# Inverse sums as powers on GpSimd, layer normalisation as scale and bias on ScalarE, and a table of orders with later hand-overs

## The reference

```python
s1 = q1 @ k1.T * scale + mask;  s2 = q2 @ k2.T * scale + mask        # 16 heads, 1024 x 1024, causal
a1, a2 = softmax(s1), softmax(s2)
lam = exp(sum(lq1 * lk1)) - exp(sum(lq2 * lk2)) + LAMBDA_INIT
out = (a1 - lam * a2) @ v                                            # per head, 64 wide
out = (out - mean) * rsqrt(var + 1e-5) * gn_w + gn_b                 # per head, over all positions
x = layernorm(x + out * (1 - LAMBDA_INIT) @ Wo)                      # (x - m) / sqrt(v + 1e-5)
x = layernorm(x + (silu(x @ wu.T) * (x @ wg.T)) @ wd.T)              # ternary wu, wg, wd
```

## Time and profile before

| | |
|---|---|
| median of 3 runs | 2446.61 us (2437.75 to 2449.0) |
| profiled execution | 2448.3 us, its span 2446.5 us |
| TensorE's mean granted clock | 0.976 of full speed |
| instructions | 41259 |
| HBM read, written | 182.53 MB, 71.30 MB, 104 GB/s over the span |
| DMA packets | 257603, mean 105 GB/s |

### The profile page before, as it was taken

How to read it: one execution, slowest core, us unless ns; L and a number is a source line. 1 busy time by engine, 2 the same in 40 slices (tenths; PEclk the granted TensorE clock), 3 DMA queues, 4 the chain that set the end, 5 groups by cost and what they waited for, 6 DMA issues and landing times.

```text
span 2446.5 us, 41259 instructions
## 1 busy us (share of the span) xinstructions
PE 2257.5 (92%) x13602; PEld 1401.3 (57%) x13602; DVE 1851.3 (76%) x4406; ACT 1417.7 (58%) x3466; POOL 860.1 (35%) x1330
## 2 busy tenths in 40 slices
PE   7799998898899999999899999999899999988999
PEld 4456655465556666666566666565565665643444
DVE  3577888888888888878788888888788888762343
ACT  1467755465556767667566766666567677640231
POOL 0344376758432323323222324324222233220132
PEclk9899999899999999999999999999999999998999
DMA  6757565466533122212622222213431211113000
GB/s 225 231 169 228 185 203 168 148 184 194 176 121 100 44 63 73 78 52 66 190 81 71 68 63 87 83 40 108 143 83 53 65 47 54 40 64 109 1 18 18
DMA packets 257603, 256.53 MB, mean 105 GB/s; under 512 B 31344, under 2 KB 199408, under 8 KB 255216
## 3 DMA queue, kind: packets, MB, share of 16 engines
q1 hardware_dynamic: 246016, 220.26, 29.8%
q10 hardware_dynamic: 11376, 33.63, 4.4%
HBM read 182.53 MB, written 71.30 MB: 104 GB/s over the span
## 4 chain that ended last, share of the span: by engine, by line
PE 66%; DVE 13%; issue 6%; POOL 6%; DMA 6%; ACT 3%; SPq 1%; ACTq 0%; DVEq 0%; POOLq 0%
PE F L994 15%; PE PV L936 9%; PE S L919 8%; PE F L1003 8%; PE F L981 8%; PE F L964 7%; PE F L904 7%; DVE e_long L1237 3%; DVE e_long L1326 3%; PE PV L939 2%; POOL coef L1170 1%; DVE e_short L1326 1%; POOL x_lo L1210 1%; PE F L972 1%; DMA wt<-in_w_up 1%
## 5 line engine op out<-in xcount | busy, mean ns | idle before, releaser
L1055 ACT ACTIVATE e_long<-e_long,nmax 128x768 f32<-128x768 f32 (+3 forms) x512 | 505.2, 989 | 148.8 <-DVE nmax L1237 144.2
L1170 POOL TENSOR_SCALAR coef<-lsum,linv,neglam 128x1 f32<-128x1 f32 x512 | 248.1, 486 | 929.4 <-DVE linv L1322 928.6
L919 PE MATMUL S<-kstk,qstk 128*128 128x384 f32 (+5 forms) x1536 | 510.1, 427 | 61.0 <-DVE nmax L1237 51.8
L1237 DVE CUSTOM_DVE_ANT_0 e_long<-S,mask_b 128x768 f32<-128x768 f32 (+3 forms) x512 | 512.7, 1018 | 68.7 <-PE S L919 64.7
L919 PEld LDWEIGHTS S<-kstk,qstk 128*128 128x128 f32 x1536 | 280.4, 195 | 208.3 <-DVE nmax L1237 89.4
L1048 ACT ACTIVATE dt_long<-F 128x512 f32<-128x512 f32 (+3 forms) x512 | 239.6, 512 | 272.8 <-PE F L904 271.9
L1326 DVE SCALAR_TENSOR_TENSOR e_long<-e_long,coef 128x1024 f32<-128x1024 f32 (+3 forms) x256 | 295.8, 1155 | 35.2 <-POOL coef L1170 34.0
L1055 ACT ACTIVATE e_short<-e_short,nmax 128x384 f32<-128x384 f32 (+3 forms) x512 | 283.3, 556 | 65.4 <-DVE nmax L1237 63.0
L964 PE MATMUL F<-xT,wr 128*128 128x512 f32 x640 | 314.5, 624 | 3.5 <-issue 0.7
L1237 DVE CUSTOM_DVE_ANT_0 e_short<-S,mask_b 128x384 f32<-128x384 f32 (+3 forms) x512 | 238.6, 486 | 44.3 <-PE S L919 43.0
L981 PE MATMUL F<-wo_sb,at_sb 128*128 128x512 f32 x512 | 240.9, 606 | 33.2 <-DMA at_sb<-da 26.4
(11 more groups left out here) (105 smaller groups left out, 3207.5 us busy)
## 6 DMA issues: line engine op xcount, KB each, us to landing
qstk<-dq SPq DMA_DIRECT2D x512, 128.0 KB, 2.8
dq<-hl SPq DMA_DIRECT2D x32, 1024.0 KB, 4.8
wr<-in_w_proj ACTq DMA_DIRECT2D x48, 512.0 KB, 4.1
kstk<-dk SPq DMA_DIRECT2D x64, 256.0 KB, 5.3
da<-ra SPq DMA_DIRECT2D x32, 512.0 KB, 3.1
at_sb<-da SPq DMA_DIRECT2D x32, 512.0 KB, 4.1
x<-in_x SPq DMA_DIRECT2D x16, 512.0 KB, 6.3
dk<-hl SPq DMA_DIRECT2D x8, 1024.0 KB, 7.0
```

The source lines that it names most:

```text
L919: last = nc.tensor.matmul(slot[:, h, :], qstk[:, duo % 4, 2 * r + m, :].bitcast(F32R), kstk[:, g % 2, m, h * w:(h + 1) * w].bitcast(F32R), ...
L1055: nc.scalar.activation(e, e, ACT.Exp, bias=nmax[:, u % 8:u % 8 + 1], scale=-1.0, accum_out=lsum[:, n % 4, m:m + 1]).then_inc(s_exp, 1)
L1170: nc.gpsimd.tensor_scalar(coef[:, a % 2:a % 2 + 1], lsum[:, a % 4, 0:1], linv[:, a % 8, 1:2], neglam[:, :], ALU.mult, ALU.mult).then_inc(s ...
L1237: nc.vector.tensor_tensor_reduce(out, slot, mask, -1.0, -NEG, ALU.add, ALU.min, nmax[:, u % 8:u % 8 + 1]).then_inc(s_negmax, 1)
```

## The change

The reciprocal of the two row sums leaves DVE. POOL's `factor` now waits for the second exponent itself, takes both sums to the power -1 (128 x 2, with the exponents from a new tile `powers`, of which `mhalf` is now the first column) and waits for its own result; then it makes the coefficient as before. `reciprocal` and its semaphore are gone. The normalisation leaves DVE too: POOL's `rsqrt` also makes bias = -mean x inverse in place of the mean, and ACT computes x x inverse + bias with `Identity`. DVE's `variance` now waits for the normalisation four tiles back, which it had behind it in its own queue before. In the tables `HAND_OVER` grows for all four engines, `factor`, `normalise` and `rsqrt` get their new durations, and the items move to their new lists.

```diff
-HAND_OVER = {"pe": 0.2, "act": 0.12, "dve": 0.1, "pool": 0.12}
+HAND_OVER = {"pe": 0.3, "act": 0.5, "dve": 0.2, "pool": 0.4}
...
     if what == "factor":
-        return 0.67 if STEPS[a].r else 0.36
+        return 1.45 if STEPS[a].r else 1.15
...
-            "lambda": 0.3, "reciprocal": 0.1, "normalise": 0.48, "high": 0.63, "product": 0.22, "moments": 1.55,
+            "lambda": 0.3, "normalise": 0.65, "high": 0.63, "product": 0.22, "moments": 1.55,
...
-            "hidden low": 1.32, "rsqrt": 1.1, "rotate": 2.9, "low": 2.6, "group": 2.9, "less": 2.9}.get(what, 0.06)
+            "hidden low": 1.32, "rsqrt": 1.5, "rotate": 2.9, "low": 2.6, "group": 2.9, "less": 2.9}.get(what, 0.06)
...
-    elif what == "reciprocal":
-        out = [ITEM("exponent", a, 1)]
...
     elif what == "factor":
-        out = [ITEM("reciprocal", a), ITEM("minus lambda")]
+        out = [ITEM("exponent", a, 1), ITEM("minus lambda")]
...
-AHEAD = {"minimum": 1.0, "exponent": 1.0, "evict": 1.5, "inverses": 1.0, "factor": 2.0, "reciprocal": 0.8, "combine": 0.6, "empty": 3.0, "copy": 2.0,
+AHEAD = {"minimum": 1.0, "exponent": 1.0, "evict": 1.5, "inverses": 1.0, "factor": 2.0, "combine": 0.6, "empty": 3.0, "copy": 2.0,
...
-        mhalf = sb("mhalf", [P, 1])
+        powers = sb("powers", [P, 4])
+        mhalf, mone = powers[:, 0:1], powers[:, 2:4]
...
+                elif what == "normalise":
+                    i = LN[a]
+                    t = a.i if a.kind == "wo" else 4 * a.h + a.j
+                    act.wait_ge(s_rstd, i + 1)
+                    nc.scalar.activation(x1[:, t, :], x1[:, t, :], ACT.Identity, bias=lmv[:, i % 4, 0:1],
+                                         scale=lrs[:, i % 4:i % 4 + 1]).then_inc(s_ln, 1)
...
-                    pool.wait_ge(s_linv, a + 1)
+                    pool.wait_ge(s_exp, 2 * a + 2)
+                    link(nc.gpsimd.tensor_tensor(linv[:, a % 8, :], lsum[:, a % 4, :], mone, ALU.pow))
...
-                    nc.gpsimd.tensor_tensor(lrs[:, i % 4:i % 4 + 1], veps, mhalf[:, :], ALU.pow).then_inc(s_rstd, 1)
+                    link(nc.gpsimd.tensor_tensor(lrs[:, i % 4:i % 4 + 1], veps, mhalf, ALU.pow))
+                    mean = lmv[:, i % 4, 0:1]
+                    nc.gpsimd.tensor_scalar(mean, mean, lrs[:, i % 4:i % 4 + 1], -1.0, ALU.mult, ALU.mult).then_inc(s_rstd, 1)
...
                 freed(dve, job)
+                if i >= 4:
+                    dve.wait_ge(s_ln, i - 3)
...
-            def normalise(job):
-                i = LN[job]
-                t = job.i if job.kind == "wo" else 4 * job.h + job.j
-                dve.wait_ge(s_rstd, i + 1)
-                nc.vector.tensor_scalar(x1[:, t, :], x1[:, t, :], lmv[:, i % 4, 0:1], lrs[:, i % 4:i % 4 + 1],
-                                        ALU.subtract, ALU.mult).then_inc(s_ln, 1)
...
-                elif what == "reciprocal":
-                    dve.wait_ge(s_exp, 2 * a + 2)
-                    nc.vector.reciprocal(linv[:, a % 8, :], lsum[:, a % 4, :]).then_inc(s_linv, 1)
```

More of the change, by code:

```diff
@@ L390 @@
             *[[ITEM("copy", j) for j in OF_KIND[kind]] for kind in ("xT", "V", "x1T", "up")],
-            [ITEM("hidden", j) for j in OF_KIND["gate"]], [ITEM("sum", i) for i in range(PREP)],
+            [ITEM("hidden", j) for j in OF_KIND["gate"]], [ITEM("normalise", j) for j in LN_JOBS], [ITEM("sum", i) for i in range(PREP)],
             [ITEM("load x", i) for i in range(len(X_JOBS) - X_FIRST)], [ITEM("load w", i) for i in range(len(WLOADS))]],
-    "dve": [[ITEM("minimum", n, m) for n, m in _maps], [ITEM("reciprocal", n) for n in _heads],
+    "dve": [[ITEM("minimum", n, m) for n, m in _maps],
             [ITEM("combine", n) for n in _heads], [ITEM("product", duo) for duo in range(DUOS)],
@@ L396 @@
               for kinds in ("EO", ("x1T",), ("up", "gate"), ("wo", "y"))],
-            [ITEM("normalise", j) for j in LN_JOBS], [ITEM("high", j) for j in O_JOBS[ROT_FIRST:]],
+            [ITEM("high", j) for j in O_JOBS[ROT_FIRST:]],
             [ITEM(what, c) for c in range(CHUNKS) for what in ("moments", "spread", "deviation")],
@@ L725, in layer_kernel @@
         s_exp = sem("s_exp")
-        s_linv = sem("s_linv")
         s_coef = sem("s_coef")
@@ L1161, in _ @@
             assert made[0] == N_CONST
-            link(nc.gpsimd.memset(mhalf[:, :], -0.5))
+            link(nc.gpsimd.memset(mhalf, -0.5))
+            link(nc.gpsimd.memset(mone, -1.0))
             pool.wait_ge(s_gn, 16)
@@ L1197, in _ @@
                     pool.wait_ge(s_gve, a + 1)
-                    link(nc.gpsimd.tensor_tensor(gsm[:, 4:5], gsm[:, 3:4], mhalf[:, :], ALU.pow))
+                    link(nc.gpsimd.tensor_tensor(gsm[:, 4:5], gsm[:, 3:4], mhalf, ALU.pow))
                     link(nc.gpsimd.tensor_tensor(gsm[:, 5:6], gsm[:, 4:5], gn_sb[:, 0, c:c + 1], ALU.mult))
@@ L1329, in _ @@
                     empty(a)
-                elif what == "normalise":
-                    normalise(a)
                 elif what == "high":
```

## The result

| | |
|---|---|
| before, beside it | 2447.38 us median of 4 runs |
| changed kernel | 2403.19 us median of 4 runs (2401.43 to 2406.22) |
| ratio | 0.9829, 95% interval 0.9801 to 0.9856 |
| predicted | 2426, range 2398 to 2464 |

The account below looks back on a forecast made before the run. TensorE was taken as the bound, busy 2257.5 of 2446.5 us. Terms -13 - 7 - 2 + 9 - 8 + 0.6 = -20.4 us took the 2446.6 us median to 2426, range 2398 to 2464 for 8 in 10.

Parts of the forecast that it names:

- VectorE's relief: TensorE's waits for VectorE shrink with its load: -13 us in 700 to 2180, -7 in 300 to 700, -2 in 76 to 300.
- The table, -8 forecast: Larger hand-over numbers remove short waits of instructions planned just in time: -8 us, bounds -20 and +15.
- under 12: Sign of being right: TensorE's waits for the row maxima in 700 to 2180 fall under 12 us.
- rival (b): No change: later coefficients take back what the minima gained, ports take 41 us of VectorE's saving; 2434 to 2459, chance 0.25.
- GpSimd, +9 forecast: In 300 to 700 GpSimd gets 75 us more, 84% busy, delaying coefficients: +28 us at most, a third taken, +9.
- the 0.64 taken: Duration in us assumed for GpSimd's power on 128x2, between bounds 0.58 and 0.88.
- rival (c): Slower: GpSimd becomes the gate in 300 to 700, comparisons of weights queue with factors; 2478 us, chance 0.20.
- 3 us are spare: Long heads' second-map loop takes 4.8 us, two heads come every 7.9; this hides the 0.45 us longer path if orders use it.
- Contention: GpSimd's powers slow VectorE operations with two SBUF inputs: 25 ns per combine taken, 13 us in all, 41 kept for the range.
- the slope of 80 ns for 17 points: Combines' lengthening with GpSimd's load, 154 ns for 34 points, gives 80 ns for the powers' 17: 41 us of VectorE.
- the forecast's upper end: Sign of being right: VectorE's busy time falls from 1851.3 us to between 1735 and 1776.
- The normalisation, part of the relief: Moving it saves VectorE 35.1 us and 14.4 of waiting; ScalarE's instruction taken at 0.77 us, 49 us in all.

Follow-up runs that it names:

- spare reciprocal: Changed kernel, lists the same, plus one unneeded one-column reciprocal on VectorE behind each second row maximum: 2406.8 us, ratio 0.9826.
- the run with the measured factor: Changed kernel with the factor planned at its profiled duration, 1.3 and 1.6 us in place of 1.15 and 1.45: 2406.3 us, ratio 0.9818.
- The multiply: Changed kernel, lists the same, with a multiply in place of GpSimd's power, so its output is not the reference's: 2386.2 us, ratio 0.9747.
- the double power: Changed kernel, lists the same, with each power on GpSimd done twice: 2525.1 us, ratio 1.0308.

## Why the prediction was right or wrong

The sign and the range held. The time fell by twice the forecast, and the largest terms stood for the wrong cause. That the waits they counted fell by 19.5 us, near their 22, is luck: the table did it, not VectorE's relief.

**The table, -8 forecast, -17 measured** alone and -20 on top of the moves (2422.7 to 2403.2). The mechanism was named in part: VectorE's idle time in front of the reciprocals fell from 87.1 us to 47.3 with the table alone. What it had wrong is which waits the table removes. It looked at those of the scores for the maxima, and they stayed (51.8 and 53.8 us). Those of the transposes for the long maps, counted under VectorE's relief, fell by 14, most of it in 300 to 700. Over the span, before and with the table alone:

```profile
PE F L904 <- DVE e_long L1326: 25.4, 24, 4.6
```

```profile
PE F L904 <- DVE e_long L1326: 11.6, 12, 2.3
```

The windows of the table-only kernel:

```profile
86.00:2100.00 2014.00, 1889.54 (x12060) 1220.07 (x12059) 1702.70 (x4153) 1332.46 (x3332) 812.58 (x1220) 0.98 0.37 111
2100.00:2428.00 328.00, 310.59 (x1350) 142.93 (x1348) 125.68 (x208) 68.77 (x108) 75.01 (x96) 0.98 0.12 38
```

The heads are 81 us shorter, with 332 matmuls less between them, and the tail is 61 longer. The other large piece lies at the seam. Before, TensorE stood still for 20.7 us behind the last head until the last chunk had gone through memory; with the table alone it waits 9.3 there and in the changed kernel 9.4, since it has filling to do meanwhile. The two rows, before and changed kernel:

```profile
PE F L981 <- DMA at_sb<-da: 20.7, 1, 20.7
```

```profile
PE F L979 <- issue: 9.4, 1, 9.4
```

This wait of 20.7 us stood in no step of the forecast, though the earlier trace rows had 27.9 us of standing still in that stretch. It shows up as well in the run without the table, at 9.7 us, so it isn't the table's alone. That is 11 us of standing still less, on a part of the path that was dismissed. How much of the 44 us it makes isn't shown: the run with normalisation and table waits only 9.4 us there too, and was 4 us faster than before.

**VectorE's relief, -13 - 7 - 2 forecast.** This step failed. It took the waits of TensorE for VectorE as a price of VectorE's load. The spare reciprocal shows the price: 80.6 us of work for at most 4 us. The waits for the maxima in 700 to 2180 are 17.5 us, not under 12, and what the powers took from them over the span came back at the maps, as rival (b) had it. Yet the parts without the table gave -24, where the forecast's terms for them make -12. Between the table-only kernel and the one with powers and table, heads take 2014 and 2022 us, and the tail 328 and 305:

```profile
82.00:2104.00 2022.00, 1906.46 (x12188) 1231.95 (x12187) 1689.10 (x3664) 1341.55 (x3350) 1167.27 (x1740) 0.98 0.37 111
2104.00:2409.00 305.00, 287.10 (x1231) 132.09 (x1228) 114.68 (x191) 59.84 (x94) 66.94 (x89) 0.97 0.13 40
```

In nearly the same time 128 more matmuls of filling stand between the heads. At fixed lists the tail doesn't move (327 to 330 us with the table's lists, 301 to 304 with the changed kernel's, whatever GpSimd does), so it is the lists that put them there. What is shown is that the gain of the power comes with the new lists and not with VectorE's time on the chip, nor with a later combine. Why the lists without reciprocals take in more filling is argued: filling needs VectorE to empty its banks, and in the scheduler's account the reciprocals took VectorE's time. It fits that setting the reciprocal's planned 0.1 us to 0 in the table-only kernel takes the planned filling behind the last scores from 313 us to 285, as with the powers (285); these are sums over the lists, and no chip ran them. That kernel, with the reciprocal still on VectorE, would have been the direct test, and it is missing. The traces leave a larger thing open. Between the table-only and the changed kernel TensorE stands still 7 us less, but its busy time is 21 us less for the same 13602 matmuls, at nearly the same granted clock (0.983 and 0.984). The profile puts 15 of the 21 at the scores (520.7 and 505.4 us); the run with the measured factor has them at 519.5 and its busy time is as low, 2240.2. So most of what the power won over the table shows in the trace as busy time, whose ends are modelled, and no run tells why.

**GpSimd, +9 forecast.** The multiply gave 17 us for 0.51 us of the path, in lists that already plan for a power; the forecast's +9 was for 0.85 us of GpSimd in 300 to 700 alone. The two aren't the same quantity, but the term was too small. The power is 0.70 us undisturbed, near the 0.64 taken and within 0.58 to 0.88; what was too small is the stretching, 0.11 us on the power and 0.07 on the coefficient. GpSimd is at 81% in 300 to 700 (84% forecast), and 94 heads pass there instead of 88 (combines 47 + 47), so rival (c) did not come. But the step "3 us are spare" was wrong: the loop over the second map was compared with the pace of the heads, and the double power, 0.85 us more, cost 122 us. The spare time of a loop belongs to the lists; what counts is how far the combine stands behind its exponent in VectorE's list. The sentence that it holds "if the orders use them" was the right condition, and the table-only lists with the power, at +57 us, show it unmet.

**Contention** was sized well where it is thin: long combines in 700 to 2180 went from 1129 to 1155 ns (25 forecast), short ones from 651 to 635. In 300 to 700, where GpSimd is full, long ones went from 1219 to 1283 and short ones from 869 to 1153, a mean of 174 ns more, twice what the slope of 80 ns for 17 points said. So VectorE ended at 1797.6 us, 22 above the forecast's upper end. The Trainium skill's GPSIMD Engine Reference (Key points) is borne out as to the shared interfaces by these combines. Its rule of thumb against elementwise work on GpSimd holds for engine time here, 0.70 us for 0.16, though power and reciprocal are not the same operation, and says nothing of the kernel's time: with VectorE's 81 us worth 4 us or less, the trade was decided by the lists.

**The normalisation, part of the relief,** is worth nothing that can be measured with the powers (2406 to 2403) and costs 13 us without them (2430 to 2443); no run tells the chip's part from that of the lists there. Its instruction takes 810 ns, where rows gave 0.68 to 0.77 and ScalarE: Activation LUTs in the Trainium skill (What ACT_TABLE_LOAD costs) 0.80: here the page was nearer than the bound from the rows.

## What to carry to other kernels

Where the instruction order comes from a scheduler's table, a change of the kernel is two changes, and they can have opposite signs: here the same move is +57 us with the old lists and -24 with its own. Price them apart, one run with the lists kept and one with the instructions kept, before naming an engine as the cause. Add up the waits after each part as well: that their sum came out as forecast hid here that another part had removed them. Cut the span where the paced part ends; how much filling is left behind it, counted in matmuls, told more than any wait.

## What the runs showed of the hardware

A power on GpSimd costs 684 ns at the least for two columns (changed kernel, line 1175) and 561 for one (kernel before, line 1187), so the second column costs about 0.12 us. A multiply of the two-column form takes 187 (median 197, run with the multiply). A reciprocal of one column on VectorE takes 157 ns, of two 160. GpSimd's small steps are stretched one by one: in the changed kernel the power's mean is 122 ns above its least duration and the coefficient behind it 77 above its least of 334, where before the coefficient alone had 155.
